# GpSimd's products of decays and G by single heads, and two waits that put it behind VectorE

## The chip, the cores and the metric

The kernel runs on one core of a Trainium2 chip. The metric is the device time of one execution in microseconds (us), from the first to the last instruction and what lies around them.

## The reference

A decoder layer runs over 64 sequences of 256 tokens with 256 features, in float32. Three parts follow each other, each with a residual and a layer norm behind it: a state space mixer (Mamba2 form), a cross attention and a coupling network.

```python
x = _layernorm(x + _L0_attn_ref(x, ...))             # mixer
x = _layernorm(x + _L0_xattn_ref(ctx_1024, x, ...))  # keys and values from context and x, queries from x
x = _layernorm(x + _L0_ffn_ref(x, ...))              # three cycles of a twisted residual
```

Two pieces matter here. In the mixer the output of each of 8 heads h is a masked product along the sequence,

```python
Lmat = jnp.exp(segsum(A))                                         # decays, a lower triangle
Y_diag = jnp.einsum('bclhn,bcshn,bhcls,bcshp->bclhp', C, B, Lmat, x)   # C.B^T is the same for all heads
```

The kernel takes the 256 tokens as one block, so that for each head it needs (exp of differences of the running sum of A) times G, where G = C.B^T. In the coupling network three cycles `out = out + coupling * twist(out)` are linear in the features of a token, so that the sum of all three is one combination of x2 and its twist with factors for each token.

## The kernel before

**A period.** The work of the three parts is laid over each other. In the loop `for p in range(2, NSEQ - 1)` (61 periods; L630 for TensorE, L1195 for ScalarE, L1929 for VectorE, L2289 for GpSimd, L2450 for the DMA queue of SyncE) a period computes the coupling network of sequence f = p - 2, the attention of a = p - 1, the mixer of m = p, and the first steps of m + 1. The order on each engine is written out by hand; engines wait for each other only by semaphores. A loop's turn in the code is the same stretch of work on all engines, but they are not at the same place of it at one time.

**The decays.** SyncE's DMA spreads the running sums of a sequence over the tile `Lm`, [128 partitions, 8 heads, 384]. GpSimd fills its triangle with -1e30 in pairs of heads (`masked(s, q)`, L2119, two instructions at L2126). ScalarE takes the exponential head by head (`decay(s, h)`, L910, which counts up `a_dec`) and copies G from PSUM to SBUF (`cb_out`, L908, semaphore `a_G`). GpSimd multiplies a pair of heads with G in one instruction of 128 x 768 (`times_g(s, q)`, L2130, the instruction at L2136). TensorE reads the pair in `y_pair(s, q)` (L325), VectorE adds x times D in `y_out(s, q)` (L1556), and TensorE's `ctxT` (L354, its transposes at L360) and the pairs 2 and 3 take the PSUM banks that `y_out` frees.

**The factors and the output.** GpSimd's `factors(s)` (L2194) computes eight small tiles for sequence s = f: the first two from the couplings of two cycles (L2204, L2205), then `e_` (L2208) from the third, and six more up to `of_x` (L2218) and `of_minus` (L2219). VectorE's `out_sum(s, i)` (L1731) makes the output of a half of the tokens from them with three instructions, L1738, L1740, L1741: a product, and two products with a sum. Their inputs lie in SBUF. `out_norm(s, i)` (the instruction at L1430) waits for the reciprocal root of the variance that GpSimd computes in `ffn(s, i)` (L2115, L2117).

**The division.** VectorE's `divide(s, d)` (L1660, L1666) multiplies half of the attention's output with the inverses of the softmax sums, which a DMA has spread over `invT`. It adds up `d_o`; TensorE's `w_o` waits for it.

**The orders around the change.** On VectorE, from the first division of a on:

```python
divide(a, 0); turn_out(a, 14); top(m, 1); gate_silu(m + 1, 0); bc(m + 1); divide(a, 1)
x_dt(m + 1, 1); top(m, 2); out_sum(f, 1); top(m, 3); top(m, 4); out_stats(f, 1); top(m, 5)
out_sum(f, 0); x2_raw(a, 0); ...; out_norm(f, 1); out_norm(f, 0); x2_raw(a, 1); x2_stats(a, 1)
turn_out(m, 0); y_out(m + 1, 0)
```

`top` (L1638) is the row maximum of scores, for which ScalarE's `exp` (L979) waits, and TensorE's scores (L428) wait for a bank that `exp` frees. `x2_raw` (L1676) frees the PSUM bank of `w_o`, which a transpose of TensorE (`turn`, L438) takes next.

Of the kernel before, what the change touches and what calls it, by code (L numbers as in the profile page):

```python
# [34 lines left out]
def decoder_layer(nc, x, xT, ctx_in, par_in, w_in, w_out, wq, wkv, wo, cw1, cw2, cw3, cw4, gw1, gw2, gw3, out):  # L35
# [4 lines left out]
    ALU, ACT, AX = mybir.AluOpType, mybir.ActivationFunctionType, mybir.AxisListType  # L40
# [3 lines left out]
    P = 128  # L44
# [7 lines left out]
    TRI = L + P  # L52
# [8 lines left out]
    with es:  # L61
        def sb(name, shape, dt=F32):
            return es.enter_context(nc.sbuf_tensor(name, shape, dt))

        def sems(*names):
            return [es.enter_context(nc.semaphore(n)) for n in names]
# [3 lines left out]
        def prm(name, i=0, rows=slice(0, P)):  # L70
# [43 lines left out]
        G = sb("G", [P, TRI])  # L114
        Lm = sb("Lm", [P, H, TRI])
# [74 lines left out]
        a_xhi, a_uB, a_u, a_thB, a_thx, a_thz, a_sp, a_G, a_dec, a_sq = sems(  # L190
            "a_xhi", "a_uB", "a_u", "a_thB", "a_thx", "a_thz", "a_sp", "a_G", "a_dec", "a_sq")
# [14 lines left out]
        d_max, d_inv, d_tn, d_o, d_x2p, d_x2, d_base = sems(  # L206
            "d_max", "d_inv", "d_tn", "d_o", "d_x2p", "d_x2", "d_base")

        d_att, (d_f,), d_ffn = sems("d_att0", "d_att1"), sems("d_f"), sems("d_ffn0", "d_ffn1")
        d_out = sems("d_out0", "d_out1")  # L210
        FD = 6

        l_mix, l_ctx, l_mask, l_Lm, l_g, l_sum, l_rms = sems(
            "l_mix", "l_ctx", "l_mask", "l_Lm", "l_g", "l_sum", "l_rms")
# [8 lines left out]
        def live(s):  # L223
            return 0 <= s < NSEQ
# [1881 lines left out]
        def _(e):  # L2106
            po = Engine(e)
            ts, tt = e.tensor_scalar, e.tensor_tensor
# [18 lines left out]
                                        channel_multiplier=-1)  # L2127
                t.then_inc(l_mask, 1)

            def times_g(s, q):  # L2130
                if not live(s):
                    return
                pair = Lm[:, 2 * q:2 * q + 2, :]
                po.wait_ge(a_dec, 8 * s + 2 * q + 2)
                po.wait_ge(a_G, s + 1)
                tt(pair, pair, G[:, :].unsqueeze(1).broadcast_to([P, 2, TRI]), ALU.mult).then_inc(l_Lm, 1)  # L2136

            def gated(s, q):
                if not live(s):
# [7 lines left out]
            def squares(s):  # L2147
                if not live(s):
                    return
                po.wait_ge(a_sq, 4 * s + 4)  # L2150
                tt(sq[:, 0:2, :], sq[:, 0:2, :], sq[:, 2:4, :], ALU.add).then_inc(l_sum, 1)
                po.wait_ge(l_sum, 2 * s + 1)
                tt(sq[:, 0, :], sq[:, 0, :], sq[:, 1, :], ALU.add).then_inc(l_sum, 1)
# [19 lines left out]
            def context(s):  # L2173
                if live(s):
                    rstd(s, "ctx", 1, J, d_ctx, l_ctx)
# [15 lines left out]
                po.wait_ge(l_tw, 2 * s + 1)  # L2191
                tt(h_b[:, :, :], h_b[:, :, :], h_a[:, :, :], ALU.subtract).then_inc(l_tw, 1)

            def factors(s):  # L2194

                if not live(s):
                    return
                n = 8 * s
                po.wait_ge(d_out[0], 3 * s)
                po.wait_ge(d_out[1], 3 * s)  # L2200
                for k in range(2):
                    po.wait_ge(c_in[k], 16 * (s + 1))
                c, d, e_ = (c_col[:, k, :] for k in range(3))
                tt(cd[:, :], c, d, ALU.mult).then_inc(l_fac, 1)  # L2204
                tt(c_d[:, :], c, d, ALU.add).then_inc(l_fac, 1)  # L2205
                po.wait_ge(d_base, s + 1)
                po.wait_ge(a_f, FA * s + 16)
                ts(e_, t_col[:, :], tf_gain[:, :], c_cyc[:, :], ALU.mult, ALU.add).then_inc(l_fac, 1)  # L2208
                po.wait_ge(l_fac, n + 3)
                ts(one_cd[:, :], cd[:, :], -1.0, 1.0, ALU.mult, ALU.add).then_inc(l_fac, 1)  # L2210
                tt(e_sum[:, :], e_, c_d[:, :], ALU.mult).then_inc(l_fac, 1)
                po.wait_ge(l_fac, n + 5)
                tt(e_one[:, :], e_, one_cd[:, :], ALU.mult).then_inc(l_fac, 1)
                po.wait_ge(l_fac, n + 6)
                tt(of_x[:, :], one_cd[:, :], e_sum[:, :], ALU.subtract)
                tt(of_tw[:, :], c_d[:, :], e_one[:, :], ALU.add).then_inc(l_fac, 1)
                po.wait_ge(l_fac, n + 7)
                ts(of_x[:, :], of_x[:, :], 1.0, None, ALU.add)  # L2218
                ts(of_minus[:, :], of_tw[:, :], -1.0, None, ALU.mult).then_inc(l_fac, 1)  # L2219
# [69 lines left out]
            for p in range(2, NSEQ - 1):  # L2289
                f, a, m = p - 2, p - 1, p  # L2290
                squares(m)
                context(m + 1)
                inv_rms(m)
                mix(m)
                twist(f)
                masked(m + 1, 0)
                masked(m + 1, 1)
                masked(m + 1, 2)
                factors(f)
                times_g(m + 1, 0)  # L2300
                masked(m + 1, 3)
                times_g(m + 1, 1)
                ffn(f, 1)
                ffn(f, 0)
                times_g(m + 1, 2)
                times_g(m + 1, 3)
                gated(m + 1, 0)
                att(a, 0)
                att(a, 1)
                gated(m + 1, 1)  # L2310
                gated(m + 1, 2)
                gated(m + 1, 3)
# [244 lines left out]
```

## Time and profile before

| what | us |
|---|---|
| median of 3 runs | 3883.71 |
| the three runs | 3893.58, 3883.71, 3880.34 |
| the profiled execution | 3894.0 |
| its span, first to last instruction | 3892.2 |
| TensorE busy in it | 3802.1 (98%) |
| VectorE busy | 3282.4 (84%) |
| ScalarE busy | 3241.6 (83%) |
| GpSimd busy | 1751.4 (45%) |

The names of engines in the profile are PE (TensorE, matmuls), PEld (TensorE, weight loads), DVE (VectorE), ACT (ScalarE), POOL (GpSimd) and SP (SyncE). A line of a timeline gives the start, the duration, the engine, the line of the kernel, the operation, output and inputs, shapes, how many instructions were merged, and in brackets how long the engine had been idle before it and what released it. A line of a stretch gives its start and end, its length, the busy time and the number of instructions of PE, PEld, DVE, ACT and POOL, TensorE's granted clock (1.00 is 2.4 GHz), the share of DMA and GB/s. Matmuls overlap, and their ends are modelled, so a PE that is busy for 98% says little of its own; gaps in it are what to look for.

### The profile page before, as it was taken

Reading aid. Unit: us, or ns where it says so; the run is one execution under the profiler, and the core shown is the slowest. Engines: PE = TensorE matmul, PEld = TensorE weight load, DVE = VectorE, ACT = ScalarE, POOL = GpSimd, SP = SyncE. Lnnn points to the kernel's source line nnn. Section 1 sums busy time; section 2 is a strip of 40 time slices with the busy share of each in tenths; the row PEclk is TensorE's granted clock in tenths of the full one; section 3 lists DMA queues with packets and bytes.
Section 4 is the critical chain, followed back from the end, with each engine's and each line's share of the span. In section 5 each row is a group of like instructions: output and inputs, shape, how many; then the busy total and the mean of one; then the engine's idle time right before and its main releaser. Section 6 shows DMA issues by size and latency. Waiting matters only on the chain.

```text
span 3892.2 us, 77180 instructions
## 1 busy us (share of the span) xinstructions
PE 3802.1 (98%) x25728; PEld 3004.2 (77%) x25728; DVE 3282.4 (84%) x8098; ACT 3241.6 (83%) x7812; POOL 1751.4 (45%) x2828
## 2 busy tenths in 40 slices
PE   6999999999999999999999999999999999999997
PEld 5777777877877777777778777777777777777775
DVE  7888888888888888888888888888888888888874
ACT  5788888888888888888888888888888888888885
POOL 3445444354454454443544544444535445444442
PEclk8999999999999999999999999999999999999998
DMA  3111112112111111121111111111211211111110
GB/s 96 54 56 49 54 44 61 54 42 59 56 44 54 55 50 54 44 61 54 42 58 57 44 54 48 57 54 44 61 51 45 57 54 48 54 46 59 54 38 17
DMA packets 312348, 203.13 MB, mean 52 GB/s; under 512 B 55056, under 2 KB 310928, under 8 KB 311952
## 3 DMA queue, kind: packets, MB, share of 16 engines
q1 hardware_dynamic: 311952, 198.20, 17.5%
q8 instruction: 206, 3.38, 0.4%
q14 instruction: 190, 1.56, 0.1%
HBM read 180.17 MB, written 17.96 MB: 51 GB/s over the span
## 4 chain that ended last, share of the span: by engine, by line
PE 59%; ACT 17%; DVE 16%; POOL 4%; issue 4%; DMA 1%; SPq 0%; DVEq 0%; POOLq 0%; ACTq 0%
PE psum L253 20%; PE psum L428 8%; PE psum L338 6%; PE psum L463 5%; PE psum L438 5%; PE psum L325 4%; PE psum L452 4%; ACT prob L979 3%; ACT h L1021 2%; ACT L979 2%; ACT L1021 2%; PE psum L497 2%; ACT xc L891 2%; POOL rs_mix L2171 2%; DVE nmax L1638 2%
## 5 line engine op out<-in xcount | busy, mean ns | idle before, releaser
L979 ACT ACTIVATE prob<-psum,nmax 128x376 f32<-128x376 f32 x1024 | 585.7, 576 | 40.1 <-DVE nmax L1638 36.7
L2136 POOL TENSOR_TENSOR Lm<-Lm,G 128x768 f32<-128x768 f32 x256 | 474.7, 1856 | 182.3 <-ACT Lm L916 127.1
L1638 DVE TENSOR_REDUCE nmax<-psum 128x1 f32<-128x376 f32 x1024 | 540.2, 538 | 14.9 <-PE psum L428 11.6
L438 PE MATMUL psum<-ident,prob 128*128 128x128 f32 (+1 forms) x3072 | 481.0, 276 | 8.7 <-DVE x L1676 6.6
L1442 DVE SCALAR_TENSOR_TENSOR u<-psum,par,u 128x253 f32<-128x253 f32 (+5 forms) x960 | 449.0, 479 | 26.6 <-ACT u L882 1.8
L428 PE MATMUL psum<-kT,q_sb 64*128 64x376 f32 x2048 | 470.5, 528 | 0.5 <-ACT prob L979 0.5
L438 PEld LDWEIGHTS psum<-ident,prob 128*128 128x128 f32 (+1 forms) x3072 | 363.5, 141 | 81.1 <-issue 43.9
L989 ACT ACTIVATE probT<-psum 128x384 f32<-128x384 f32 x512 | 253.0, 494 | 190.2 <-PE psum L438 189.9
L2126 POOL TENSOR_SCALAR_AFFINE_SELECT Lm<-Lm 128x256 f32<-128x256 f32 x512 | 205.8, 437 | 412.3 <-DMA Lm<-cum_row 412.3
L253 PE MATMUL psum<-x_hi,w_in_hi 128*128 128x256 f32 (+1 forms) x1152 | 358.6, 311 | 19.5 <-DVE w_in_lo L1764 9.3
L452 PE MATMUL psum<-probT,V 128*64 128x256 f32 (+1 forms) x3072 | 374.9, 385 | 0.3 <-ACT probT L989 0.3
L253 PE MATMUL psum<-x_hi,w_in_lo 128*128 128x256 f32 (+1 forms) x1152 | 326.3, 283 | 0.0
L253 PE MATMUL psum<-x_lo,w_in_hi 128*128 128x256 f32 (+1 forms) x1152 | 325.9, 283 | 0.0
L1657 DVE COPY probT<-psum 128x384 f32<-128x384 f32 x512 | 279.6, 546 | 42.9 <-PE psum L438 41.5
L452 PEld LDWEIGHTS psum<-probT,V 128*64 128x64 f32 (+1 forms) x3072 | 202.3, 136 | 134.8 <-ACT probT L989 33.1
L2190 POOL TENSOR_TENSOR h_a<-h_a,cpl 128x512 f32<-128x512 f32 x64 | 82.1, 1283 | 492.3 <-DVE h_pre L1724 492.3
L915 ACT ACTIVATE Lm<-Lm,ncum 128x256 f32<-128x256 f32 x512 | 262.2, 512 | 0.7 <-DVE ncum L1533 0.7
L463 PE MATMUL psum<-wo_sb,oT 128*128 128x256 f32 x1024 | 248.2, 385 | 0.7 <-DVE oT L1666 0.7
L979 ACT ACT_TABLE_LOAD x189 | 242.5, 1283 | 3.4
L253 PEld LDWEIGHTS psum<-x_hi,w_in_hi 128*128 128x128 f32 (+1 forms) x1152 | 215.1, 187 | 35.0 <-issue 20.1
L338 PE MATMUL psum<-w_out_sb,g 128*128 128x256 f32 x1024 | 237.3, 385 | 0.0
L463 PEld LDWEIGHTS psum<-wo_sb,oT 128*128 128x128 f32 x1024 | 188.9, 189 | 59.1 <-issue 33.0
(222 smaller groups left out, 11179.2 us busy)
## 6 DMA issues: line engine op xcount, KB each, us to landing
Lm<-cum_row SPq DMA_DIRECT2D x64, 1024.0 KB, 5.1
Lm<-cum_row SPq DMA_DIRECT2D x64, 512.0 KB, 6.5
invT<-inv_row SPq DMA_DIRECT2D x256, 128.0 KB, 3.0
xT_sb<-in_xT SPq DMA_DIRECT2D x64, 256.0 KB, 3.3
x_sb<-in_x SPq DMA_DIRECT2D x64, 256.0 KB, 3.6
result<-out_sb SPq DMA_DIRECT2D x64, 256.0 KB, 2.2
inv_row<-inv_t SPq DMA_DIRECT2D x512, 1.0 KB
ctx_sb<-in_ctx SPq DMA_DIRECT2D x64, 120.0 KB, 2.4
```

The lines of the kernel that those rows point to most:

```text
L253: t = mm(dst, a, b, start=n == 1, stop=n == 3 * KT)
L338: t = mm(banks[b][:, i * D:(i + 1) * D], g[:, c, i * P:(i + 1) * P], w_out_sb[:, c, :], start=c == 0, stop=c == CT - 1)
L428: mm(banks[b][:, 0:NK], q_sb[r, c, i * P:(i + 1) * P], kT[r, c, :], start=True, stop=True).then_inc(p_sc, 1)
L438: t = tr(banks[b][0:m, j * P:(j + 1) * P], prob[:, r, j0:j0 + m], ident[:, :])
L452: t = mm(banks[b][k * HD:(k + 1) * HD, 0:L], V[0:m, j, h * HD:(h + 1) * HD], probT[0:m, (8 * s + h) % HP, j, :], start=j == 0, stop=j == l ...
L463: t = mm(banks[b][:, 0:D], oT[:, c, i * P:(i + 1) * P], wo_sb[:, c, :], start=c == 0, stop=c == CT - 1)
L915: act(Lm[:, h, 0:L], Lm[:, h, 0:L], ACT.Exp, bias=ncum[:, 0, h:h + 1])
L979: act(prob[:, r, :], b[:, 0:NK], ACT.Exp, bias=nmax[:, n:n + 1], accum_out=psum_row[:, n:n + 1]).then_inc(a_exp, 1)
L1442: stt(u[0:rows, c, d:L], src[:, 0:L - d], prm("conv_w", 4 * c + 3 - d, slice(0, rows)), u[0:rows, c, d:L], ALU.mult, ALU.add).then_inc(don ...
L1638: e.tensor_reduce(nmax[:, n:n + 1], banks[bank_of["sc", s, n]][:, 0:NK], AX.X, ALU.max, negate=True).then_inc(d_max, 1)
L1657: cp(probT[:, (8 * s + 2 * c + k) % HP, :, i * P:(i + 1) * P], b[:, 0:len(JT) * P].rearrange("p (j t) -> p j t", j=len(JT))).then_inc(d_tn, 1)
L2136: tt(pair, pair, G[:, :].unsqueeze(1).broadcast_to([P, 2, TRI]), ALU.mult).then_inc(l_Lm, 1)
```

## The change

`times_g` multiplies each head of the pair by itself, with an instruction of 128 x 384 that waits for the decay of this head alone; only the second counts up `l_Lm`. With `summed=f` the first of the two waits for VectorE's last instruction of `out_sum(f, 1)`. `factors` with `divided=a` waits for `divide(a, 1)` ahead of `e_`. Both arguments are given in the loop alone, to `factors(f)` and to the call of `times_g` behind it.

```diff
-            def times_g(s, q):
+            def times_g(s, q, summed=None):
+
                 if not live(s):
                     return
-                pair = Lm[:, 2 * q:2 * q + 2, :]
-                po.wait_ge(a_dec, 8 * s + 2 * q + 2)
+                if summed is not None:
+                    po.wait_ge(d_out[1], 3 * summed + 3)
                 po.wait_ge(a_G, s + 1)
-                tt(pair, pair, G[:, :].unsqueeze(1).broadcast_to([P, 2, TRI]), ALU.mult).then_inc(l_Lm, 1)
+                for h in (2 * q, 2 * q + 1):
+                    po.wait_ge(a_dec, 8 * s + h + 1)
+                    t = tt(Lm[:, h, :], Lm[:, h, :], G[:, :], ALU.mult)
+                t.then_inc(l_Lm, 1)
...
-            def factors(s):
+            def factors(s, divided=None):
...
                 po.wait_ge(d_base, s + 1)
                 po.wait_ge(a_f, FA * s + 16)
+                if divided is not None:
+                    po.wait_ge(d_o, 2 * divided + 2)
                 ts(e_, t_col[:, :], tf_gain[:, :], c_cyc[:, :], ALU.mult, ALU.add).then_inc(l_fac, 1)
...
-                factors(f)
-                times_g(m + 1, 0)
+                factors(f, divided=a)
+                times_g(m + 1, 0, summed=f)
```

The order on GpSimd from `factors` to the first root of `ffn(f, 1)` stood so before (c_col is the tile of the couplings, `e_` one of its columns; the lines of `factors` are L2204 to L2219):

```order
L2204 TENSOR_TENSOR cd<-c_col 128x2 [waits c_in0,c_in1,d_out1,d_out0]
L2205 TENSOR_TENSOR c_d<-c_col 128x2
L2208 TENSOR_SCALAR c_col<-t_col,tf_gain,c_cyc 128x2 [waits a_f,d_base]
L2210 TENSOR_SCALAR one_cd<-cd 128x2 [waits l_fac]
...
L2219 TENSOR_SCALAR of_minus<-of_tw 128x2
L2136 TENSOR_TENSOR Lm<-Lm,G 128x768 [waits a_G,a_dec]
L2126 AFFINE_SELECT Lm<-Lm 128x2x128 x2
L2136 TENSOR_TENSOR Lm<-Lm,G 128x768 [waits a_dec]
L2115 TENSOR_SCALAR ve_ffn<-mv_ffn 128x1 [waits d_ffn1]
```

and with the change, where the lines of `factors` are L2209 to L2226 and the product is L2139:

```order
L2209 TENSOR_TENSOR cd<-c_col 128x2 [waits c_in1,c_in0,d_out0]
L2210 TENSOR_TENSOR c_d<-c_col 128x2
L2215 TENSOR_SCALAR c_col<-t_col,tf_gain,c_cyc 128x2 [waits d_o,a_f,d_base]
L2217 TENSOR_SCALAR one_cd<-cd 128x2 [waits l_fac]
...
L2226 TENSOR_SCALAR of_minus<-of_tw 128x2
L2139 TENSOR_TENSOR Lm<-Lm,G 128x384 [waits a_dec,a_G,d_out1]
L2139 TENSOR_TENSOR Lm<-Lm,G 128x384 [waits a_dec]
L2126 AFFINE_SELECT Lm<-Lm 128x2x128 x2
L2139 TENSOR_TENSOR Lm<-Lm,G 128x384 [waits a_dec] x2
L2115 TENSOR_SCALAR ve_ffn<-mv_ffn 128x1 [waits d_ffn1]
```

The sequence of the work is the same: one product of 768 columns is two of 384, and there are two new semaphores, d_o ahead of `e_` and d_out1 ahead of the first product. On the other engines nothing moves.

## Rows read from the trace of the kernel before

**Rows 1.** Stretches, busy time by engine, clock: 60 periods, and one plain period (A)

```profile
167.71:3735.67 3567.96, 3539.06 (x24124) 2801.37 (x24122) 3065.12 (x7561) 3033.77 (x7321) 1639.57 (x2640) 1.00 0.18 52
704.06:763.14 59.08, 58.85 (x406) 46.60 (x404) 50.73 (x127) 50.50 (x123) 27.14 (x45) 1.00 0.19 53
```

**Rows 2.** Stretches: one of seven long periods (B), and the seven together

```profile
763.14:824.45 61.31, 59.16 (x406) 46.82 (x404) 53.47 (x127) 50.62 (x123) 27.00 (x44) 1.00 0.18 50
...
sum 434.58, PE 418.00 PEld 329.95 DVE 374.30 ACT 355.20 POOL 190.40; mean PE 59.71 PEld 47.14 DVE 53.47 ACT 50.74 POOL 27.20
```

**Rows 3.** Timeline of VectorE in period B, which starts at 763.14

```profile
782.98 1.98 DVE L1741 SCALAR_TENSOR_TENSOR out_sb<-x,of_minus,out_sb 128x128 f32<-128x128 f32 x1
...
792.21 1.90 DVE L1430 TENSOR_SCALAR out_sb<-out_sb,mv_ffn,rs_ffn 128x256 f32<-128x256 f32 x1 [0.46 <-POOL rs_ffn L2117]
794.03 0.41 DVE L1676 TENSOR_TENSOR x<-psum,x 128x256 f32<-128x256 f32 x1
...
795.49 0.47 DVE L1556 SCALAR_TENSOR_TENSOR xc<-xc,par,psum 128x256 f32<-128x256 f32 x1
```

**Rows 4.** Timeline of GpSimd in period B

```profile
783.01 1.81 POOL L2136 TENSOR_TENSOR Lm<-Lm,G 128x768 f32<-128x768 f32 x1 [0.72 <-ACT G L908]
...
792.14 3.64 POOL L2136 TENSOR_TENSOR Lm<-Lm,G 128x768 f32<-128x768 f32 x2
796.04 0.74 POOL L2145 TENSOR_TENSOR g<-xc,gate 128x256 f32<-128x256 f32 x1 [0.26 <-DVE xc L1556]
```

**Rows 5.** Timeline of TensorE in period B: its two gaps

```profile
794.50 0.54 PE L438 MATMUL psum<-ident,prob 128*120 128x128 f32 x3 [0.95 <-DVE x L1676]
796.02 0.43 PE L360 MATMUL psum<-ident,ctx_n 120*128 120x120 f32 x2 [0.98 <-DVE xc L1556]
```

**Rows 6.** Timeline of VectorE in period A, which starts at 704.06

```profile
720.65 0.69 DVE L1666 TENSOR_TENSOR oT<-oT,invT 128x512 f32<-128x512 f32 x1
...
723.89 0.35 DVE L1741 SCALAR_TENSOR_TENSOR out_sb<-x,of_minus,out_sb 128x128 f32<-128x128 f32 x1
...
726.75 0.34 DVE L1741 SCALAR_TENSOR_TENSOR out_sb<-x,of_minus,out_sb 128x128 f32<-128x128 f32 x1
...
731.49 0.41 DVE L1430 TENSOR_SCALAR out_sb<-out_sb,mv_ffn,rs_ffn 128x256 f32<-128x256 f32 x1 [0.46 <-POOL rs_ffn L2117]
...
733.60 0.48 DVE L1556 SCALAR_TENSOR_TENSOR xc<-xc,par,psum 128x256 f32<-128x256 f32 x1 [0.24 <-PE psum L325]
```

**Rows 7.** Timeline of GpSimd in period A

```profile
720.74 0.82 POOL L2208 TENSOR_SCALAR c_col<-t_col,tf_gain,c_cyc 128x2 f32<-128x2 f32 x1 [3.03 <-ACT t_col L1029]
...
723.96 1.95 POOL L2136 TENSOR_TENSOR Lm<-Lm,G 128x768 f32<-128x768 f32 x1 [0.76 <-ACT G L908]
...
727.76 1.84 POOL L2136 TENSOR_TENSOR Lm<-Lm,G 128x768 f32<-128x768 f32 x1 [1.09 <-ACT Lm L916]
...
730.86 0.59 POOL L2117 TENSOR_TENSOR rs_ffn<-ve_ffn,minus_half 128x1 f32<-128x1 f32 x1
731.82 3.77 POOL L2136 TENSOR_TENSOR Lm<-Lm,G 128x768 f32<-128x768 f32 x2 [0.37 <-ACT Lm L916]
```

**Rows 8.** Timeline of TensorE in period A: the transposes of the context, no gap before them

```profile
734.51 0.37 PE L360 MATMUL psum<-ident,ctx_n 120*128 120x120 f32 x2
```

**Rows 9.** One line's instructions, durations min/median/max in ns: shorter products of GpSimd

```profile
L2145 POOL TENSOR_TENSOR g<-xc,gate x256: 725/740/1194, 41.6 to 3771.7; 128x256 f32<-128x256 f32 x128
...
L2151 POOL TENSOR_TENSOR gate<-gate x64: 1268/1294/1307, 54.3 to 3774.5; 128x512 f32<-128x512 f32 x64
```

**Rows 10.** Timeline of GpSimd in period C, which starts at 285.83

```profile
302.50 0.34 POOL L2208 TENSOR_SCALAR c_col<-t_col,tf_gain,c_cyc 128x2 f32<-128x2 f32 x1 [2.57 <-ACT t_col L1029]
...
308.33 0.88 POOL L2126 TENSOR_SCALAR_AFFINE_SELECT Lm<-Lm 128x256 f32<-128x256 f32 x2
```

**Rows 11.** Timeline of VectorE in period C: from `out_sum(f, 0)`

```profile
308.57 0.37 DVE L1740 SCALAR_TENSOR_TENSOR out_sb<-x,of_tw,out_sb 128x128 f32<-128x128 f32 x1
```

**Rows 12.** Stretches: the sum over seven periods whose second division was late, C among them

```profile
sum 417.11, PE 415.12 PEld 327.93 DVE 356.94 ACT 353.85 POOL 190.32; mean PE 59.30 PEld 46.85 DVE 50.99 ACT 50.55 POOL 27.19
```

## The prediction

> **What bounds the kernel now.** I read the shares of busy time first: TensorE is the bound. Then I cut the span at GpSimd's instruction L2190, which runs once in a period, and had the stretches listed. From 167.71 to 3735.67 lie 60 periods in 3567.96 us, 59.47 each, though the plain one has 59.08 [rows 1]. Seven are long, 434.58 us together [rows 2], and seven more a little long, 417.11 together [rows 12]. What is left is 3567.96 - 434.58 - 417.11 = 2716.27 us in 46 periods, or 59.05. So the seven long ones cost 434.58 - 7 x 59.05 = 21.2 us, and the other seven 417.11 - 413.35 = 3.8 us. In a plain period TensorE is busy for 58.85 of 59.08 us at the full clock [rows 1]: nothing on the other engines can make it shorter. What there is to gain lies in the long ones.
>
> Next I laid the timelines of a long period (B) over those of a plain one (A, 59.08 us before B). They are alike up to VectorE's last instruction of `out_sum(f, 1)`. In B it takes 1.98 us [rows 3] where A has 0.35 [rows 6], and it ends just behind GpSimd's product of a pair, which started 0.03 us after it (783.01 against 782.98) [rows 3, 4]. In A the same product started 0.07 us after it (723.96 against 723.89) and took 1.95 us where 1.81 is usual: there GpSimd gave way [rows 4, 6, 7]. So this is a race of some hundredths of a microsecond between ScalarE's copy of G, which releases the product, and VectorE. The loser stands until the winner's instruction is over. The seven long periods all lost it.
>
> A lost race costs VectorE 1.6 us, and then a second one follows. In A there are 0.37 us between GpSimd's last root of `ffn` and its next product, as that waits for ScalarE's decays [rows 7], and VectorE's second `out_norm` slips in at 731.49. In B the decays are ready, the product starts at 792.14, and `out_norm` at 792.21 takes 1.90 us for 0.41 [rows 3, 4, 6]. Both delays reach TensorE as two gaps, 0.95 us behind `x2_raw` (L1676) and 0.98 us behind `y_out` (L1556) [rows 5].
>
> **The change, part by part.**
>
> *The wait for the output sum.* The first product now starts behind L1741. It can't lose VectorE 1.6 us there any more, in any period. Price on GpSimd below.
>
> *The wait for the division.* In A `e_` starts at 720.74 while the division runs (720.65 to 721.34), and stretches to 0.82 us, up to 721.56 [rows 6, 7]. With nothing beside it, it takes 0.34 us [rows 10]. Now it starts 0.08 us behind the division (as L2145 starts 0.08 us behind L1556 in B [rows 3, 4]), so at 721.42, and ends at 721.76: 0.20 us later than before. All six that follow, and `out_sum(f, 1)` and the row maxima behind it, are 0.20 us later. In B 1.6 us of delay at this place gave no gap of TensorE until 794.50 [rows 3, 5]. So I cost it at nothing of its own; the delay is carried on below. Where the division comes late for its DMA, `e_` comes late with it. There the period slides as a whole, as the row maximum behind the division does already, so that the 3.8 us of those seven stay.
>
> *Single heads.* A product of 256 columns takes 0.74 us and one of 512 takes 1.29 [rows 9], the pair of 768 some 1.82 [rows 4]. Between the first two lies 1.01 us for 384 columns. Two are 2.02 us, 0.2 more than the pair; four pairs make 0.8 us more work for GpSimd in a period, which is busy for 27 of 59 us [rows 1].
>
> *The sum along GpSimd in period A.* L1741 ends at 723.89 + 0.35 + 0.20 = 724.44. Head 0 runs 724.52 to 725.53, head 1 to 726.54, the two masks to 727.4 (0.88 us where VectorE's sums run beside them, in period C [rows 10]). Head 2 need not wait for the decay of head 3, for which the pair waited until 727.76 [rows 7]: it runs 727.4 to 728.4, head 3 to 729.4. The pair ended at 729.60. So the two roots of `ffn` come 0.2 us earlier, the second ends at 731.45 - 0.2 = 731.25, and head 4, whose decay is long there, follows at once. The gap of 0.37 us is gone. So **the second race is now lost in every period**: `out_norm` wants to start at 731.29 and stands until head 4 is done at 732.26. In B the next instruction of VectorE started 0.07 us after the pair that ran in its way, so `x2_raw` starts at 732.33.
>
> *What TensorE feels of that.* From `x2_raw` to `y_out` it is 795.49 - 794.03 = 1.46 us in B with no idle time [rows 3]. So `y_out` starts at 733.79, against 733.60 in A, where it had idled 0.24 us [rows 6]. TensorE's L360 came 796.02 - 795.49 = 0.53 us after that start in B [rows 3, 5]; in A it starts at 734.51 without a gap [rows 8]. So `y_out` may start at 733.98 before TensorE waits, and it is in time by **0.19 us**. That is the narrow place of this forecast. The other wait has more room: L438 started 0.47 us after `x2_raw` in B, so could start at 732.80, and it lies 0.54 us long just ahead of L360, at 733.97. The plain period stays at 59.05.
>
> *Outside the loop* the first three sequences have single heads too; the nearest row is the 0.2 us more for a pair, and heads that waited for their pair may start sooner. Between +1 and -1 us, taken as 0.
>
> **The sum**: 3894.0 (the profiled execution) - 21.2 = 3872.8 us. The profiled execution is 10.3 us over the median of 3883.71 and 0.4 over the slowest run. I take it that the runs differ mostly in how many races they lose (3.0 us each), and that without them all come to about the same, so that the forecast holds for the median too. Against that median it is -0.28%, right at the 0.3% (11.7 us) which a measurement of this kernel can tell from no change.
>
> **Rivals.**
>
> *1, slower: each side stands for the other in turn.* In the new order GpSimd's head 1, the masks and head 2 run without a break beside the three instructions of `out_sum(f, 0)` (L1738, L1740, and L1741 at about 727). If each of them waits for a whole instruction of the other engine, and then the other for it, some 0.25 us of VectorE's work come three times between GpSimd's: head 2 starts about 0.8 us later than I have it, and so do the roots, head 4 and `y_out`. Then TensorE waits 0.8 - 0.19 = 0.6 us in every period, 60 x 0.6 = 36 us: 3909. It decides from 0.19 us on: at half the delay it is 60 x 0.2 = 12 us, 3885. Against it speaks period C, where the masks lay beside the sums as they will now: L1740 ran under the first of them and took 0.37 us, against 0.35 for L1741 in A [rows 6, 10, 11]. But there was no product right behind them.
> The Trainium skill ("SBUF — State Buffer", Who interferes with whom) states that a VectorE instruction with two SBUF inputs and a GpSimd instruction that reads SBUF exclude each other, and that the one that issues second fully blocks. The trace agrees for the products (1.98 and 1.90 us). For the masks it does not: by the page L1740 would have stood until the mask was over, and its row has 0.37 us. By the page the time is that of this rival, 3909; by the row it is the forecast.
>
> *2, no change: the race moves.* Head 2 starts at about 727.4 by my sum, and L1741 of `out_sum(f, 0)` at 727.1 (726.75 in A [rows 6], later by the 0.20 and, as an estimate, 0.15 for head 1 and the masks beside it). If in part of the periods the product is there first, VectorE loses up to 1.0 us, less than the 1.6 now, as the product is shorter; it then meets head 4 later than above and pays some 0.5 us on TensorE. In a third of the periods that is 20 x 0.5 = 10 us: 3883, no change to the median. For it speaks that my times are good to about 0.1 us and the margin is 0.3.
>
> *3, no change: long periods have another root.* If both are late for a third thing and the long L1741 is only where it shows, they stay, at about 3884 to 3894. Against it: L1741 starts 19.84 us into B and 19.83 into A, the product 19.87 and 19.90 [rows 3, 4, 6, 7]; there is nothing else to tell them apart there.
>
> **How the numbers follow.** Forecast 0.64; rival 1 0.17 (0.12 of it near the full price, the rest at half); rival 2 0.15; rival 3 0.04. Within the forecast the time lies in 3867 to 3879, and the bound of 3872.1 cuts it near the middle: 0.34 faster by over 0.3%, 0.30 within. Rival 1 gives same 0.05 and slower 0.12, rival 2 same 0.12 and slower 0.03, rival 3 same 0.03 and slower 0.01. Together: faster 0.34, same 0.50, slower 0.16. The range starts at 3866 (the 3.8 us of the late divisions go too, the start gives 1 us, and 2 for the spread) and goes to 3893, which takes in rival 2, the cheap part of rival 1 and most of rival 3.
>
> **What would show it.** Right: the first product of a period (L2139) always starts behind L1741, and no L1741 or L1430 over 1.2 us; `e_` (L2215) at 0.34 us instead of 0.82; the second `out_norm` at about 1.0 us in nearly all periods instead of 0.41; no period near 61 to 63 us, and 59.05 for the plain ones. Wrong by rival 1: L360 waits for L1556 in every period, which then is 59.2 or longer. Wrong by rival 2: an L1741 of 1.0 to 1.2 us in some periods, with L360's wait in the same ones.

## The result, and the profile after

The changed kernel took 3864.69 us (median; 3862.73 to 3865.99), the one before 3883.71: a ratio of 0.9946, 95% interval 0.9931 to 0.9961. That is 0.54% faster, outside the 0.3% that can be told from no change, and under the low end of the range I had given (3866). The profiled execution took 3863.23 us, its span 3861.4. The median fell by 19.0 us and the profiled execution by 30.8, because the profiled execution of the kernel before lay 10.3 us over its median; the parts below add up to the 30.8.

Stretches of the changed kernel, cut as in [rows 1], at its L2194: the 60 periods, a plain one, and one of nine that are longer. Columns as there.

```profile
167.64:3704.97 3537.33, 3520.09 (x24124) 2798.49 (x24122) 3067.39 (x7561) 3030.04 (x7321) 1634.90 (x2880) 1.00 0.18 53
934.98:993.80 58.82, 58.62 (x406) 46.66 (x404) 51.09 (x127) 50.46 (x123) 27.15 (x48) 1.00 0.18 53
875.15:934.98 59.83, 58.80 (x406) 46.61 (x404) 51.19 (x127) 50.58 (x123) 27.58 (x48) 1.00 0.18 52
...
sum 536.74, PE 530.69 PEld 420.55 DVE 461.62 ACT 454.78 POOL 245.57; mean PE 58.97 PEld 46.73 DVE 51.29 ACT 50.53 POOL 27.29
```

The last line is the sum over the nine longer periods, 59.15 to 59.86 each. The other 51 have (3537.33 - 536.74) / 51 = 58.83 us (they are the plain ones), against 59.05 before. So the 3567.96 - 3537.33 = 30.6 us that the loop lost come in three parts:

| part | us |
|---|---|
| the seven lost races of L1741 | -21.2 |
| the plain period, 60 x (58.83 - 59.05) | -13.2 |
| late transfers and what follows, 536.74 - 9 x 58.83 = 7.3 instead of 3.8 | +3.5 |

That adds up to -30.9; the difference of the profiled executions is 30.8. Outside these 60 periods the span changed by 0.2 us.

The groups of VectorE's three instructions in question and of `e_`, with min/median/max in ns:

```profile
L1741 DVE SCALAR_TENSOR_TENSOR out_sb<-x,of_minus,out_sb x128: 343/348/1419, 187.8 to 3855.7; 128x128 f32<-128x128 f32 x128
L1430 DVE TENSOR_SCALAR out_sb<-out_sb,mv_ffn,rs_ffn x128: 381/416/1092, 194.0 to 3858.5; 128x256 f32<-128x256 f32 x128
L1438 DVE TENSOR_TENSOR x_lo<-xT_sb,x_hi x64: 683/687/1237, 5.1 to 3680.2; 128x512 fp32r<-128x512 f32 x64
L2215 POOL TENSOR_SCALAR c_col<-t_col,tf_gain,c_cyc x64: 341/342/344, 185.1 to 3852.1; 128x2 f32<-128x2 f32 x64
its engine sat idle before it (us, times) until:
  DVE oT L1666: 223.6, 61
```

One L1741 of 1.42 us is left; it lies behind the loop and was there before too. The second `out_norm` (L1430) now takes 1.08 us in each of 61 periods. Both as forecast. What I had not looked at is the third row: the same group before the change, in VectorE's `x_low` (L1438), had a median of 1.04 us:

```profile
L1438 DVE TENSOR_TENSOR x_lo<-xT_sb,x_hi x64: 683/1037/1049, 5.3 to 3710.7; 128x512 fp32r<-128x512 f32 x64
```

`x_low` makes the low part of the next sequence's input, for which TensorE's projection L253 waits. It has two inputs in SBUF. Its surroundings in period A of the kernel before (which starts at 704.06), VectorE, GpSimd, TensorE:

```profile
738.15 1.04 DVE L1438 TENSOR_TENSOR x_lo<-xT_sb,x_hi 128x512 fp32r<-128x512 f32 x1
...
737.91 2.65 POOL L2145 TENSOR_TENSOR g<-xc,gate 128x256 f32<-128x256 f32 x3
...
738.47 0.87 PE L438 MATMUL psum<-ident,prob 128*120 128x128 f32 x6
739.34 0.32 PE L253 MATMUL psum<-x_hi,w_in_hi 128*80 128x256 f32 x1
```

and in a plain period of the changed kernel (from 934.98), with the stretch of GpSimd that leads there:

```profile
951.57 0.69 DVE L1666 TENSOR_TENSOR oT<-oT,invT 128x512 f32<-128x512 f32 x1
...
952.47 0.34 POOL L2215 TENSOR_SCALAR c_col<-t_col,tf_gain,c_cyc 128x2 f32<-128x2 f32 x1 [3.84 <-DVE oT L1666]
...
955.57 1.96 POOL L2139 TENSOR_TENSOR Lm<-Lm,G 128x384 f32<-128x384 f32 x2 [1.12 <-DVE out_sb L1741]
957.49 0.87 POOL L2126 TENSOR_SCALAR_AFFINE_SELECT Lm<-Lm 128x256 f32<-128x256 f32 x2
958.33 2.01 POOL L2139 TENSOR_TENSOR Lm<-Lm,G 128x384 f32<-128x384 f32 x2
...
962.16 3.94 POOL L2139 TENSOR_TENSOR Lm<-Lm,G 128x384 f32<-128x384 f32 x4
...
968.42 2.65 POOL L2149 TENSOR_TENSOR g<-xc,gate 128x256 f32<-128x256 f32 x3
...
962.22 1.08 DVE L1430 TENSOR_SCALAR out_sb<-out_sb,mv_ffn,rs_ffn 128x256 f32<-128x256 f32 x1 [0.46 <-POOL rs_ffn L2117]
963.23 0.41 DVE L1676 TENSOR_TENSOR x<-psum,x 128x256 f32<-128x256 f32 x1
...
964.68 0.47 DVE L1556 SCALAR_TENSOR_TENSOR xc<-xc,par,psum 128x256 f32<-128x256 f32 x1
...
969.02 0.69 DVE L1438 TENSOR_TENSOR x_lo<-xT_sb,x_hi 128x512 fp32r<-128x512 f32 x1
...
969.34 0.87 PE L438 MATMUL psum<-ident,prob 128*120 128x128 f32 x6
969.96 0.36 PE L253 MATMUL psum<-x_hi,w_in_hi 128*80 128x256 f32 x1
```

`x_low` is issued at the same place of the period, 34.09 before and 34.04 after. Before, the three gated products of GpSimd start 0.24 us ahead of it and the first of them holds it up. After, they start 0.60 us ahead, since head 4 follows the root at once (962.16, which is 27.18; before the pair waited for its decays until 27.76 [rows 7]). `x_low` takes 0.35 us less and is through 0.40 us sooner, and L253 starts at 34.98 of the period instead of 35.28. Before L253 there is no gap in either trace, and yet it waits in one of them. The last of the six transposes ahead of it (L438), before and then after:

```profile
739.07 0.27 PE L438 MATMUL psum<-ident,prob 128*128 128x128 f32 x1
...
969.93 0.27 PE L438 MATMUL psum<-ident,prob 128*128 128x128 f32 x1
```

Before, L253 starts 0.27 us behind the start of that transpose, just where its drawn end lies (738.47 + 0.87 = 739.34), and 0.15 us behind the end of `x_low`. After, it starts 0.03 us behind the start of the transpose, 0.25 us ahead of its drawn end, and 0.26 us behind the end of `x_low`: it no longer waits for `x_low`. The wait shows only as an overlap that is missing.

In seven of the nine longer periods the input transfer is late and TensorE waits 0.3 to 0.8 us at L253; in the other two (from 285.80 and 1230.02) it is the second division that is late. In the one shown above (875.15), ScalarE's copy waits for it, `x_low` meets the next gated product and loses again, and now TensorE shows a gap:

```profile
908.79 0.63 ACT L849 ACTIVATE x_hi<-xT_sb 128x512 fp32r<-128x512 f32 x1 [0.90 <-DMA xT_sb<-in_xT]
...
910.02 1.04 DVE L1438 TENSOR_TENSOR x_lo<-xT_sb,x_hi 128x512 fp32r<-128x512 f32 x1
...
911.21 0.32 PE L253 MATMUL psum<-x_hi,w_in_hi 128*80 128x256 f32 x1 [0.81 <-DVE x_lo L1438]
```

### The profile page after: what moved, and what is told of

Its sections match the earlier page's. It is cut to its first block, busy times and chain, and to the rows that moved or that the text cites. A ratio compares the mean times of both kernels' runs of the same rounds, so it can differ in the third digit from the quotient of the medians.

```text
span 3861.4 us, 77375 instructions
## 1 busy us (share of the span) xinstructions
PE 3783.3 (98%) x25728; PEld 3000.9 (78%) x25728; DVE 3286.2 (85%) x8098; ACT 3237.9 (84%) x7812; POOL 1748.5 (45%) x3084
## 4 chain that ended last, share of the span: by engine, by line
PE 59%; ACT 16%; DVE 15%; issue 4%; POOL 4%; DMA 1%; SPq 0%; DVEq 0%; POOLq 0%
PE psum L253 20%; PE psum L428 8%; PE psum L338 6%; PE psum L463 5%; PE psum L438 5%; PE psum L452 4%; PE psum L325 4%; ACT prob L979 3%; ACT h L1021 2%; ACT L979 2%; ACT L1021 2%; PE psum L497 2%; ACT xc L891 2%; POOL rs_mix L2175 2%; DVE nmax L1638 1%
## 5 line engine op out<-in xcount | busy, mean ns | idle before, releaser
L2139 POOL TENSOR_TENSOR Lm<-Lm,G 128x384 f32<-128x384 f32 x512 | 506.1, 1012 | 92.8 <-DVE out_sb L1741 68.4
L438 PE MATMUL psum<-ident,prob 128*128 128x128 f32 (+1 forms) x3072 | 480.5, 276 | 2.1 <-ACT probT L989 1.1
L438 PEld LDWEIGHTS psum<-ident,prob 128*128 128x128 f32 (+1 forms) x3072 | 363.0, 141 | 73.9 <-issue 45.0
L253 PE MATMUL psum<-x_hi,w_in_hi 128*128 128x256 f32 (+1 forms) x1152 | 360.9, 313 | 22.5 <-DVE w_in_lo L1764 9.3
L253 PE MATMUL psum<-x_hi,w_in_lo 128*128 128x256 f32 (+1 forms) x1152 | 326.0, 283 | 0.0
L253 PE MATMUL psum<-x_lo,w_in_hi 128*128 128x256 f32 (+1 forms) x1152 | 325.4, 283 | 0.0
L2194 POOL TENSOR_TENSOR h_a<-h_a,cpl 128x512 f32<-128x512 f32 x64 | 82.0, 1281 | 492.3 <-DVE h_pre L1724 492.3
L253 PEld LDWEIGHTS psum<-x_hi,w_in_hi 128*128 128x128 f32 (+1 forms) x1152 | 215.0, 187 | 28.4 <-issue 12.8
```

Source lines behind the costliest of these rows:

```text
L253: t = mm(dst, a, b, start=n == 1, stop=n == 3 * KT)
L438: t = tr(banks[b][0:m, j * P:(j + 1) * P], prob[:, r, j0:j0 + m], ident[:, :])
L2139: t = tt(Lm[:, h, :], Lm[:, h, :], G[:, :], ALU.mult)
```

## The experiments

My theory after the result: the plain period is shorter because `x_low` no longer stands behind a gated product, and that comes from where the single heads put GpSimd, not from less work or from a wait. The rivals: the two waits shorten it, or the products that TensorE gets sooner. Experiments 1 to 4, 5 to 8 and 9 to 11 were measured on three different chips, with the kernel before beside them at 3891.86, 3885.95 and 3907.08 us. The changed kernel took 3864.69 us in the first comparison and 3865.55 in 9, so a ratio from one group is not to be compared with one from another; the plain periods can be.

### 1. The two waits alone

The changed kernel with the pair of 768 columns:

```diff
-                for h in (2 * q, 2 * q + 1):
-                    po.wait_ge(a_dec, 8 * s + h + 1)
-                    t = tt(Lm[:, h, :], Lm[:, h, :], G[:, :], ALU.mult)
-                t.then_inc(l_Lm, 1)
+                pair = Lm[:, 2 * q:2 * q + 2, :]
+                po.wait_ge(a_dec, 8 * s + 2 * q + 2)
+                tt(pair, pair, G[:, :].unsqueeze(1).broadcast_to([P, 2, TRI]), ALU.mult).then_inc(l_Lm, 1)
```

> The two waits of the change stay, the products are pairs of 768 columns again. Theory (x_low): the changed kernel's plain period of 58.82 us instead of 59.05 comes from VectorE's x_low (L1438), which took 1.04 us before, behind GpSimd's gated product, and 0.69 us after, since GpSimd comes to the gated products 0.4 us earlier; and that comes from the single heads alone (head 4 waits for no decay of head 5). Then here x_low is at 1.04 us again and the plain period at 59.05; the races lost by L1741 are gone all the same, so the time is what I had forecast for the whole change: 3873 us, between 3869 and 3878. Rival (the waits make the plain period shorter, by keeping GpSimd off the division and the output sum): plain period near 58.8, 3860 to 3867 us, whatever x_low takes.

Measured: 3939.64 us, ratio to before 1.0125 (1.0107 to 1.0143). Neither was right: the waits alone make the kernel 1.25% slower. The plain period is 60.06 us. Its timeline (it starts at 528.53), VectorE, GpSimd, TensorE:

```profile
556.26 1.94 DVE L1430 TENSOR_SCALAR out_sb<-out_sb,mv_ffn,rs_ffn 128x256 f32<-128x256 f32 x1 [0.46 <-POOL rs_ffn L2117]
...
552.54 1.84 POOL L2139 TENSOR_TENSOR Lm<-Lm,G 128x768 f32<-128x768 f32 x1 [0.85 <-ACT Lm L916]
...
556.23 3.74 POOL L2139 TENSOR_TENSOR Lm<-Lm,G 128x768 f32<-128x768 f32 x2
...
560.11 0.42 PE L360 MATMUL psum<-ident,ctx_n 120*128 120x120 f32 x2 [0.97 <-DVE xc L1556]
```

The second race of my prediction, now lost in every period and at the full width of a pair: `out_norm` is issued 0.03 us behind it and takes 1.94 us, and TensorE waits 0.97 us for `y_out`. The wait for the division is what brings `out_norm` there: it makes `e_`, the output sum and, by the row maxima, the decays of heads 2 and 3 some 0.3 us later, so the second pair, the roots and `out_norm` too, which comes at 27.73 of the period instead of 27.43. The pair of heads 4 and 5 is not later (27.70 against 27.76 in period A), and is now there first.

### 2. Single heads alone

The changed kernel with `factors(f)` and `times_g(m + 1, 0)`, neither wait.

> The products are single heads, neither wait is there. Theory (x_low): x_low at 0.69 us and the plain period at 58.82 as with the whole change. The first product can run into L1741 again, but the lost race costs VectorE some 0.8 us instead of 1.6, as a head takes 1.0 us; 5 to 20 of the 60 periods lose it (7 of 60 with pairs), and since the second out_norm loses in every period already, a lost one costs 0 to 0.8 us of the period: 3863 to 3878 us, likeliest 3868. Rival (the waits make the plain period shorter): plain period 59.05 and 3873 or more.

Measured: 3873.34 us, ratio 0.9955 (0.994 to 0.9971). The race with L1741 is lost in nearly every period (59 of the 60), not in 5 to 20, as the head starts 0.03 us ahead of L1741. VectorE and GpSimd in a plain period (from 524.13):

```profile
543.94 1.12 DVE L1741 SCALAR_TENSOR_TENSOR out_sb<-x,of_minus,out_sb 128x128 f32<-128x128 f32 x1
...
543.91 2.00 POOL L2139 TENSOR_TENSOR Lm<-Lm,G 128x384 f32<-128x384 f32 x2 [0.67 <-ACT G L908]
...
558.23 0.80 DVE L1438 TENSOR_TENSOR x_lo<-xT_sb,x_hi 128x512 fp32r<-128x512 f32 x1
...
557.75 2.65 POOL L2149 TENSOR_TENSOR g<-xc,gate 128x256 f32<-128x256 f32 x3
```

It costs 0.8 us of VectorE each time, and yet the plain period is 58.90, for a lost 0.8 us is covered at this place. `x_low` starts 0.48 us behind the gated products and takes 0.80.

### 3. The kernel before, with `x_low` guarded

One wait is added to the kernel before, in the loop alone:

```diff
-            def gated(s, q):
+            def gated(s, q, behind=None):
                 if not live(s):
                     return
+                if behind is not None and live(behind):
+                    po.wait_ge(d_xlo, behind + 1)
...
-                gated(m + 1, 1)
+                gated(m + 1, 1, behind=m + 2)
```

> The kernel before (pairs, no new waits) with one wait more: the gated products 1 to 3 of a sequence start behind x_low of the next one. Theory (x_low): x_low takes 0.69 us instead of 1.04, TensorE's projection behind it (L253) starts 0.3 us earlier and the plain period is 58.82 instead of 59.05, 13 us in all; the long periods with an L1741 of 2 us stay, so some 3870 us against 3884 before. Rival (TensorE gains because the products of the decays are ready earlier, or through anything else ahead of the gated products): plain period stays at 59.05 and the time at 3884. A third way: the gated products, which end 0.8 us later, become a wait of their own, and the period is longer.

Measured: 3873.98 us (3863.47 to 3881.1), ratio 0.9955 (0.9938 to 0.9972). `x_low` never takes more than 0.69 us, and the plain period is 58.82, that of the changed kernel, with pairs and without its waits:

```profile
521.56:580.38 58.82, 58.61 (x406) 46.59 (x404) 50.52 (x127) 50.45 (x123) 26.81 (x45) 1.00 0.18 53
```

The groups of `x_low` and L1741, and GpSimd's gated products in that period:

```profile
L1438 DVE TENSOR_TENSOR x_lo<-xT_sb,x_hi x64: 680/685/693, 5.2 to 3697.0; 128x512 fp32r<-128x512 f32 x64
...
L1741 DVE SCALAR_TENSOR_TENSOR out_sb<-x,of_minus,out_sb x128: 335/344/1981, 188.3 to 3873.6; 128x128 f32<-128x128 f32 x128
```

```profile
556.37 2.26 POOL L2147 TENSOR_TENSOR g<-xc,gate 128x256 f32<-128x256 f32 x3 [0.98 <-DVE x_lo L1438]
```

GpSimd stands 0.98 us for it and nobody misses the gated products. The long L1741 stay, seven in the loop of this execution. So the 0.23 us a period come back with the order of `x_low` and the gated products alone.

### 4. The changed kernel, with the gated products 0.4 us later

```diff
+                for n in range(2):
+                    ts(pads[:, n, :], minus_half[:, 0:2], 1.0, None, ALU.mult)
                 gated(m + 1, 1)
```

> The changed kernel with two small instructions of GpSimd more (128x2, written to a tile of their own, some 0.2 us each) between the second root of att and gated product 1, so that only gated products 1 to 3 come 0.4 us later, where they stood before the change. Theory (x_low): x_low loses again, about 1.0 us, and the plain period is back at 59.05: 3878 us (3874 to 3880). Rival (another root of the shorter period): plain period stays at 58.82, 3865 us.

Measured: 3879.01 us, ratio 0.9972 (0.9961 to 0.9983); plain period 59.12. A new tile shifts the lines by one. VectorE, then GpSimd:

```profile
556.90 1.14 DVE L1439 TENSOR_TENSOR x_lo<-xT_sb,x_hi 128x512 fp32r<-128x512 f32 x1
...
556.39 0.42 POOL L2319 TENSOR_SCALAR pads<-minus_half 128x2 f32<-128x2 f32 x2
556.77 2.64 POOL L2150 TENSOR_TENSOR g<-xc,gate 128x256 f32<-128x256 f32 x3
```

Two small instructions, 0.42 us a period on an engine that is busy for less than half of it, cost 14 us. The heads are as in the change and TensorE gets them at the same time, so that rival falls.

### 5. Pairs with the wait for the output sum alone

As in 1, with `factors(f)`.

> Pairs of 768 columns, no wait for the division, only the wait of the first product for VectorE's output sum (L1741). Theory: what made the version with both waits and pairs slow (plain period 60.04) is the wait for the division: e_ and with it the output sum, the roots and VectorE's second out_norm come 0.33 us later, at 27.76 in the period, just behind the pair that starts at 27.71 when its decays are there, and out_norm stands for the whole pair (1.92 us). Here out_norm is back at 27.41 and wins, x_low loses as before the change (1.04 us), and only the long L1741 are gone: plain period 59.05, no period over 61, 3873 us (3869 to 3877). Rival (the wait for the sum is what pushes the pairs into out_norm): out_norm over 1.2 us in most periods and 3890 to 3940.

Measured: 3872.32 us (its profiled execution 3876.12), ratio 0.997 (0.9957 to 0.9984); plain period 59.04, no long L1741 in the loop, `out_norm` never over 0.42 us, `x_low` 1.04. This is what I had forecast for the whole change (3872.8): the sum over the races was right, and the wait for the output sum alone gives it.

### 6. Head 4 waits for the decay of head 5

```diff
-                    po.wait_ge(a_dec, 8 * s + h + 1)
+                    po.wait_ge(a_dec, 8 * s + (h if q != 2 else 5) + 1)
```

> The changed kernel, but head 4 waits for the decay of head 5 as the pair did (heads 5 to 7 as in the change). Theory: the 0.4 us by which GpSimd comes earlier to its gated products are this wait; with it head 4 starts near 27.7 in the period instead of 27.18, the second out_norm (issued at 27.24) wins and takes 0.41, the gated products come at 31.5 and 33.85, x_low loses again (about 1.04) and the plain period is back at 59.05 to 59.1: 3878 us (3874 to 3882). Rival (the second lost race or the shorter instructions themselves are what moved the period): plain period 58.82 and 3865, or below it as out_norm is short.

Measured: 3879.57 us, ratio 0.9985 (0.9973 to 0.9997); plain period 59.14. GpSimd and VectorE (from 524.09):

```profile
551.84 3.90 POOL L2139 TENSOR_TENSOR Lm<-Lm,G 128x384 f32<-128x384 f32 x4 [0.56 <-ACT Lm L916]
...
558.06 2.65 POOL L2149 TENSOR_TENSOR g<-xc,gate 128x256 f32<-128x256 f32 x3
...
551.32 0.42 DVE L1430 TENSOR_SCALAR out_sb<-out_sb,mv_ffn,rs_ffn 128x256 f32<-128x256 f32 x1 [0.46 <-POOL rs_ffn L2117]
...
558.17 1.16 DVE L1438 TENSOR_TENSOR x_lo<-xT_sb,x_hi 128x512 fp32r<-128x512 f32 x1
```

`out_norm` wins its race and `x_low` loses: VectorE gets 0.66 us back at the first and pays 0.47 at the second, and the kernel is slower than the changed one by some 15 us. The 0.56 us that head 4 no longer waits is where the gain of the plain period comes from: it brings the gated products forward.

### 7. Without the wait for the division

> The changed kernel without the wait for the division. Theory: e_ stretches to 0.82 us beside the division again but ends 0.33 us earlier, so the output sum, the first product (20.26 instead of 20.59) and the roots do too; x_low wins anyway, TensorE sees nothing of it: plain period 58.82, 3865 us (3861 to 3868), the wait for the division being worth nothing here. Rival (without it the order of some other pair of instructions flips): one of VectorE's instructions longer in most periods and 3870 or more.

Measured: 3870.23 us, ratio 0.996 (0.9948 to 0.9972), 5.5 us over the changed kernel; plain period 58.97. My theory (worth nothing) was wrong and the rival right: one of VectorE's instructions is longer in most periods, and it is `x_low` again. VectorE, then GpSimd's gated product 1, and 2 and 3 (from 523.38):

```profile
557.43 1.00 DVE L1438 TENSOR_TENSOR x_lo<-xT_sb,x_hi 128x512 fp32r<-128x512 f32 x1
...
556.47 0.73 POOL L2149 TENSOR_TENSOR g<-xc,gate 128x256 f32<-128x256 f32 x1
...
557.15 1.87 POOL L2149 TENSOR_TENSOR g<-xc,gate 128x256 f32<-128x256 f32 x2
```

All of GpSimd is 0.35 us earlier, so product 1 is past, but product 2 has begun 0.28 us ahead of `x_low` and holds it up in its place. The changed kernel puts `x_low` just on the seam between products 1 and 2. Side by side, the medians over the 60 periods, the lead being that of the product that runs when `x_low` is issued, and the third column the median of the sum:

| kernel | lead of the gated product | `x_low` | lead + duration | plain period |
|---|---|---|---|---|
| changed | 0.60 | 0.69 | 1.28 | 58.84 |
| single heads alone (2) | 0.47 | 0.81 | 1.28 | 58.90 |
| no wait for the division (7), product 2 | 0.27 | 1.00 | 1.27 | 58.97 |
| before | 0.24 | 1.04 | 1.27 | 59.06 |
| padded (4) | 0.16 | 1.12 | 1.27 | 59.12 |
| head 4 late (6) | 0.11 | 1.16 | 1.27 | 59.14 |

`x_low` ends 1.28 us behind the start of the product that was first, whenever it is issued. It loses some 0.59 us less the lead. The period doesn't follow that loss evenly, but the start of L253 behind the start of the last L438: 0.03 us in the changed kernel and in every version with the guard, 0.04 in 2, 0.24 in 7, 0.27 before, 0.35 in 4 and 0.40 in 6 (medians over the plain periods). The last four have plain periods 0.13, 0.22, 0.28 and 0.30 us longer than the changed kernel. So the first 0.1 us that `x_low` loses are free, and the 0.06 us of 2 are hardly its doing; where they come from isn't shown.

### 8. The changed kernel with `x_low` guarded

The edit of 3 on the changed kernel.

> The changed kernel, with gated products 1 to 3 behind x_low of the next sequence. Theory: x_low wins in the plain periods already, so they stay at 58.82; in the six or seven where x_low is late (for its own input's transfer), it lost 0.35 us more to a gated product, which goes: 2 to 3 us in all, 3862 us (3859 to 3866). Rival (the gated products, some 0.7 to 1.4 us later, are waited for): plain period longer, 3870 or more.

Measured: 3861.68 us (3861.14 to 3862.3), ratio 0.9937 (0.9919 to 0.9956). The plain period is the same, 58.83. This was as expected.

### 9 to 11. Three versions on one chip

The changed kernel again; the pairs of 5 with the guard; the kernel of 7 with the guard.

> The changed kernel once more, unaltered, so that the next versions stand beside it on the same chip: 3865 us (3862 to 3867).

> Pairs of 768 columns, the first behind VectorE's output sum; no wait for the division; gated products 1 to 3 behind x_low. Theory: the single heads and the wait for the division do nothing of their own, they only move GpSimd's gated products along the clock, past x_low. With x_low guarded by a wait, pairs give the same plain period of 58.82, and with the races of L1741 gone the time is that of the changed kernel with this guard, 3862 us (3859 to 3866). Rival (single heads are needed for the short period): 59.0 and 3872.

> The changed kernel without the wait for the division and with gated products 1 to 3 behind x_low. Theory: without the wait for the division x_low took 1.00 us because gated product 1 ran 0.35 us earlier and product 2 stood in x_low's way in its place (start of product 1 33.09, of x_low 34.05); the lost time is 0.6 us less the lead of the product that runs. So with the guard the plain period is 58.82 again and the time 3862 us (3859 to 3866). Rival (the missing wait costs by e_ beside the division): plain period 58.97, 3868 to 3872.

Measured, with six runs each and the kernel before at 3907.08 us beside them:

| kernel | median us (lowest to highest) | ratio to before | plain period |
|---|---|---|---|
| changed, again | 3865.55 (3864.83 to 3865.87) | 0.9888 (0.9864 to 0.9911) | 58.83 |
| pairs, wait for the sum, guard | 3862.14 (3860.83 to 3863.85) | 0.9879 (0.9853 to 0.9905) | 58.85 |
| single heads, wait for the sum, guard | 3862.02 (3860.65 to 3863.11) | 0.9878 (0.9855 to 0.9902) | 58.85 |

With `x_low` guarded, it makes no difference whether there are pairs or single heads (10 against 11), nor, with single heads, whether there is a wait for the division (8 against 11). Pairs with both waits and the guard were not run: the guard does nothing for the `out_norm` that experiment 1 lost in every period, 1.0 us each time. The runs of the two guarded versions all lie below those of the changed kernel, by 3.4 and 3.5 us at the median; the intervals against the kernel before overlap.

### 12. The kernel before, profiled again

> The kernel before, unaltered, profiled once more. Its runs beside the experiments lie between 3871 and 3932 us, those of the changed kernel between 3863 and 3866. Theory: the spread is the number N of periods in which the first product of a pair gets ahead of VectorE's L1741 (1.98 us there), each with 2.3 us here and the second lost race behind it, 3.0 us in all: the profiled time is 3873 + 3.0 N, with N counted by the L1741 of more than 1.5 us. Rival (the spread comes from something else, as late transfers): N stays at 7 whatever the time.

Measured: 3884.61 us (3879.78 to 3895.69), the profiled execution 3888.85. In it five of the loop's L1741 took over 1.5 us, so 3873 + 5 x 3.0 = 3888 was expected; with seven it had been 3894.0. The first of them, with the lost `out_norm` behind it:

```profile
1252.31 1.98 DVE L1741 SCALAR_TENSOR_TENSOR out_sb<-x,of_minus,out_sb 128x128 f32<-128x128 f32 x1
...
1261.52 1.90 DVE L1430 TENSOR_SCALAR out_sb<-out_sb,mv_ffn,rs_ffn 128x256 f32<-128x256 f32 x1 [0.46 <-POOL rs_ffn L2117]
```

Two counts fit, but the 3.0 us are an average, and not split as expected. Three of the seven long periods of the first profile take 61.32 to 61.36 us, so both lost races together cost 2.3; the other four take 62.26 to 62.92, and in them `x_low` starts at 37.3 to 38.2 of the period instead of 36.6. The five of this profile are one of the first kind and four of the second. Why `x_low` is so late in those four isn't shown. That the runs of the kernel before at 3907 and 3932 us lost 11 and 20 such races would follow from this average, but was not seen, as no such run was profiled.

## Why the prediction was wrong, step by step

- **The lost races: right.** "The seven long ones cost 21.2 us": with the wait for the output sum alone (5) the kernel took 3872.32, where I had put 3872.8. Of the 21.2 some 16 are the price of the two lost races themselves (7 x 2.3), the rest goes with the late `x_low` of four of those periods (12). That all runs come to about the same without the races held too: the changed kernel's lie within 3.3 us in the first comparison, those of the kernel before within 13.
- **The wait for the division: the delay was mis-sized, and its price had the wrong sign.** `e_` starts 0.21 us behind the division (952.26 to 952.47), not 0.08, so the output sum is 0.33 us later and not 0.20. I cost it at nothing. It is worth some -5 us with single heads (7), +1.0 us a period with pairs (1 against 5), and nothing with single heads once `x_low` is guarded (8 against 11).
- **Single heads: right.** 1.01 us was the estimate and 1012 ns the mean; the two masks took 0.87 for 0.88, head 4 started at 27.18 for 27.19. That last agreement is partly luck: head 0 came 0.13 us later than I had it (20.59 for 20.46 of the period), and this was made up as two heads in a row take 1.96 us and not 2.02, and the masks start before the second has ended.
- **The second race: right, in every period.** `out_norm` 1.08 us for "about 1.0", `x2_raw` at 28.25 for 28.27, `y_out` at 29.70 for 29.73, and TensorE did not wait. With a pair in place of head 4 (1) it waited 0.97 us: the narrow place was where I said.
- **The step that failed:** "In a plain period TensorE is busy for 58.85 of 59.08 us at the full clock: nothing on the other engines can make it shorter." The changed kernel's plain period has TensorE busy for 58.62 of 58.82 us with the same work. The busy time holds hidden waits, as the ends of matmuls are modelled: before, TensorE's L438 is drawn up to the start of L253 while L253 waits 0.24 us for `x_low`, and without that wait the two overlap. So I didn't look at any instruction that is lost in every period, only at what sets long periods off from plain ones, and that comparison can't show `x_low`, which lost in both. I had worked out that head 4 moves forward by 0.6 us and followed it up to `y_out`, not to GpSimd's next instructions, the gated products, and to what they stand in the way of. It's 13.2 of the 30.8 us: with it and the 3.5 us of the next point the sum comes to 3872.8 - 13.2 + 3.5 = 3863.1, and the profiled execution took 3863.23.
- **The late periods:** "the 3.8 us of those seven stay" was 7.3 us in this execution: 1.4 in the two periods with a late division alone, and 5.9 in the seven with a late input, for which I had no term. Where the input is late, `x_low` loses at least 0.35 us again. The guard (8) took 3.0 us off, 2.4 of which it should by this count; how many transfers are late differs from one execution to the next (3.2 to 7.1 us over 60 plain periods in the single head versions without the guard but with the wait for the sum).
- **The rivals.** 1: the masks and the sums did not stand for each other in turn. L1740 took 0.37 us beside a mask; L1741 of `out_sum(f, 0)`, which starts beside the second mask, took 0.49 us for 0.34 in every period, and that cost no time. The rule of the Trainium skill ("SBUF — State Buffer", Who interferes with whom), by which each would have stood until the mask was over, is not what the masks' rows show. The rows of the products beside L1741 and `x_low`, which have two inputs in SBUF, agree with it: `x_low` takes 1.04 us when issued 0.24 us behind a gated product and 0.69 when ahead of it. (`out_norm`, whose 1.90 us I had counted to that rule too, reads one tensor and two columns of scalars; it is held up all the same.) Had I applied it (an instruction of VectorE with two inputs in SBUF and one of GpSimd that reads SBUF exclude each other) to every such pair in a plain period, I would have come upon L1438. 2: the race did not move to `out_sum(f, 0)`: no L1741 in the loop took 1.0 us. 3: fell, as no long period was left once the first product stood behind L1741 (5).

## What to carry to other kernels

Where two engines exclude each other, moving either one shifts all its later instructions too: list every instruction of the other engine that stands in a race, in plain periods too, with its duration alone and beside its rival, and follow the move up to the last of them. A high busy share of TensorE does not show that it never waits; compare the start of an instruction with the end of what it depends on and with the start of the instruction ahead of it. A gain that hangs on 0.1 us of alignment is better pinned by a wait: here one semaphore wait of GpSimd gave the 0.23 us a period that the change had by the place where its heads happened to end, and kept them with pairs and with single heads. It is no guard for the other races: each critical instruction needs its own.

## What was not expected of the hardware

- The price of a lost race is a straight line: `x_low` ends 1.28 us behind the start of GpSimd's 256-column product, for leads from 0.11 to 0.60 us. The product itself is shown as 0.73 us, but stands in the way for 0.59.
- `e_`, which waits for VectorE's division, starts 0.21 us behind its end, while L2145 started 0.08 us behind L1556. The distance is not the same for all pairs.
- The single head started 0.03 us ahead of L1741 and the pair 0.03 behind it (2 against [rows 3, 4]). ScalarE's copy of G came 0.05 us earlier in the period in 2; where the rest comes from the traces don't show.
